# A selective-scan block with a quantised layer on one core: the direct sums of a unit ordered chunk by chunk instead of state by state

## The reference

```python
def _selective_scan(xc, delta, A, Bm, Cm, D_skip):
    dA = jnp.exp(delta[..., None] * A)
    dBx = (delta * xc)[..., None] * Bm[:, :, None, :]
    def step(h, inp):
        dA_t, dBx_t, C_t = inp
        h = dA_t * h + dBx_t
        y_t = jnp.einsum('bds,bs->bd', h, C_t)
        return (h, y_t)
    ...
    return y + D_skip * xc
...
delta = jax.nn.softplus(x_conv @ W_dt + b_dt)
y = _selective_scan(x_conv, delta, A, Bm, Cm, D_skip)
y = y * jax.nn.silu(z)
out = y @ W_out + b_out
return _layernorm(residual + out, alpha, beta)
```

## Time and profile before

| | |
|---|---|
| time, median of 3 runs | 615.03 us (614.58 to 618.79) |
| the profiled execution | 615.47 us, span of the core 613.7 us, mean granted clock of TensorE 0.94 |
| TensorE busy | 521.3 us |
| VectorE busy | 506.9 us |
| ScalarE busy | 437.3 us |
| GpSimd busy | 333.5 us |
| direct sums L1291, L1288 | 160 of 0.473 us, 32 of 0.483 us (median) |
| transposes of the states L1063 | 1024 of 0.273 us (median) |

### The profile page before, as it was taken

The page is one execution under the profiler, slowest core; times in us unless marked ns, Lnnn a source line. Parts: engine busy times, 40 slices in busy tenths (PEclk is TensorE's granted clock), DMA queues, the critical chain, the costliest instruction groups (busy, mean ns, idle before and its releaser), DMA issues.

```text
span 613.7 us, 10300 instructions
## 1 busy us (share of the span) xinstructions
PE 521.3 (85%) x2885; PEld 399.3 (65%) x2885; DVE 506.9 (83%) x1010; ACT 437.3 (71%) x882; POOL 333.5 (54%) x332
## 2 busy tenths in 40 slices
PE   7998999998999879988999789988998786962292
PEld 4566787876687757766777658776877575752031
DVE  4357799888889879898989978889989999885585
ACT  3569884988398947987598639895889586801364
POOL 3054365567365837656666735584847666501154
PEclk9999999998899999999999989999999999877555
DMA  7203351145213440445024601343053505530018
GB/s 192 49 1 69 70 104 36 36 87 102 52 27 78 91 84 1 81 90 103 1 43 98 121 15 35 68 99 73 1 103 69 103 1 103 108 66 0 1 41 200
DMA packets 20066, 41.43 MB, mean 68 GB/s; under 512 B 3760, under 2 KB 10032, under 8 KB 20016
## 3 DMA queue, kind: packets, MB, share of 16 engines
q0 software_dynamic: 10080, 35.13, 29.1%
q1 hardware_dynamic: 9936, 5.78, 3.6%
HBM read 3.68 MB, written 2.10 MB: 9 GB/s over the span
## 4 chain that ended last, share of the span: by engine, by line
PE 44%; DVE 19%; POOL 12%; issue 11%; ACT 10%; DVEq 1%; DMA 0%; POOLq 0%; ACTq 0%
PE drive L1047 14%; PE hT L1063 10%; DVE state L1268 7%; PE fbank L983 6%; PE fbank L1001 4%; DVE acc_d L1291 3%; ACT decay L785 2%; ACT nrm L696 2%; POOL u L511 2%; ACT term L806 2%; PE bbank L1081 2%; PE drive L1044 2%; POOL state L662 1%; PE drive L983 1%; PE fbank L990 1%
## 5 line engine op out<-in xcount | busy, mean ns | idle before, releaser
L1268 DVE TENSOR_TENSOR_SCAN state<-decay,drive 128x512 f32<-128x512 f32 x256 | 297.2, 1201 | 23.7 <-PE drive L1047 13.6
L785 ACT ACTIVATE decay<-delta,a_neg 128x510 f32<-128x510 f32 x256 | 170.5, 731 | 46.4 <-DVE state L1268 44.6
L1047 PE MATMUL drive<-diag,uT 128*128 128x256 f32 x768 | 186.3, 387 | 0.8 <-DVE uT L1488 0.8
L1063 PE MATMUL hT<-ident,state 128*128 128x128 f32 x1024 | 146.3, 280 | 31.2 <-DVE acc_d L1291 21.7
L1063 PEld LDWEIGHTS hT<-ident,state 128*128 128x128 f32 x1024 | 119.1, 144 | 64.0 <-issue 25.2
L1047 PEld LDWEIGHTS drive<-diag,uT 128*128 128x128 f32 x768 | 141.3, 194 | 17.6 <-DVE uT L1488 1.0
L806 ACT ACTIVATE term<-hT,Ct 128x256 f32<-128x256 f32 x256 | 102.7, 485 | 5.0 <-PE hT L1063 3.5
L538 POOL TENSOR_SCALAR_AFFINE_SELECT diag<-Bt 128x512 f32<-128x512 f32 x96 | 65.6, 713 | 34.3 <-PE drive L1047 17.5
L1291 DVE SCALAR_TENSOR_TENSOR acc_d<-hT,Ct,acc_d 128x256 f32<-128x256 f32 x160 | 66.5, 470 | 4.6 <-PE hT L1063 4.5
L523 POOL TENSOR_TENSOR scaled<-uT,Bt 128x1024 f32<-128x1024 f32 x32 | 65.5, 2048 | 8.3 <-DVE uT L1488 4.2
L554 POOL DMA_DIRECT2D acc<-term x64 | 59.9, 936 | 7.6 <-ACT term L806 6.3
(11 more groups left out here) (188 smaller groups left out, 688.1 us busy)
## 6 DMA issues: line engine op xcount, KB each, us to landing
acc<-term POOLq DMA_DIRECT2D x64, 512.0 KB, 4.5
out_dram<-x_all SPq DMA_DIRECT2D x7, 256.0 KB, 3.0
x_all<-term POOLq DMA_DIRECT2D x6, 256.0 KB, 4.1
x_all<-in_L_attn_x_dram SPq DMA_DIRECT2D x2, 256.0 KB, 4.0
state<-in_L_attn_conv_w_dram SPq DMA_DIRECT2D x1, 512.0 KB, 5.8
w_in<-in_L_attn_W_in_dram SPq DMA_DIRECT2D x1, 256.0 KB, 4.6
w_dt<-in_L_attn_W_dt_dram SPq DMA_DIRECT2D x1, 256.0 KB, 4.5
out_dram<-x_all SPq DMA_DIRECT2D x2, 128.0 KB, 2.8
```

The costliest lines, as they stand in the source:

```text
L785: last = nc.scalar.activation(decay[:, g % DECAYS, h, :, s, 1:], delta[:, par, h, :, 1:], ACT.Exp, scale=a_neg[:, h, SG * g + s:SG * g + s ...
L1047: last = nc.tensor.matmul(dst[:, :, P * c:P * c + P], uT[:, par, TC * b + c, P * h:P * h + P], diag[:, n % DIAGS, c, :, :], start=True, st ...
L1063: last = nc.tensor.transpose(hT[:, c, DI * s + P * h:DI * s + P * h + P], state[:, n % STATES, h, s, P * c:P * c + P], ident[:, :])
L1268: nc.vector.tensor_tensor_scan(state[:, n % STATES, h, :, :].rearrange("p s t -> p (s t)"), decay[:, g % DECAYS, h, b, :, :].rearrange("p ...
```

## The change

VectorE's loop over the four sums of a direct unit is turned: chunk outside, state inside. The four instructions of a unit were state 0 of chunk 0, state 0 of chunk 1, state 1 of chunk 0, state 1 of chunk 1; they become state 0 and state 1 of chunk 0, then state 0 and state 1 of chunk 1. The function directs, which tells the count at which each is done, is turned in the same way. So TensorE's wait at L1058 before bank 0 (state SG - 1, chunk 0) ends with the second sum of the unit in place of the third, and before bank 1 with the fourth as it did. VectorE's own wait at L1290 for state 0 of the same chunk now names the instruction directly in front; before, one instruction stood between. The wait for the second bank's transposes (L1286) stands before the third sum in place of the second. Everything else is as it was.

```diff
 def directs(j, s, c):
 
-    return 2 * TC * j + TC * s + c + 1
+    return 2 * TC * j + SG * c + s + 1
...
                 if j == 0 and pr.after(1):
                     dve.wait_ge(ysum_ready, nth(pr.plus(-1), PAIR, 0))
-                for s in range(SG):
-                    for c in range(TC):
+                for c in range(TC):
+                    for s in range(SG):
                         a = acc_d[:, par, b, c, :]
                         src = hT[:, c, DI * s:DI * s + DI]
                         by = Ct[:, par, TC * b + c, SG * g + s:SG * g + s + 1]
```

## The result

The changed kernel takes 624.22 us (median of 4 runs, 623.28 to 625.56) where the kernel before took 615.06 (4 runs): 1.0137 times as long, 95% interval 1.0103 to 1.0171. The forecast was 617.0 with a range of 612.0 to 620.5; the change costs 9.2 us instead of 2. The profiled execution took 625.15 us, span 623.4.

A forecast was written before the change was run, and what follows sets the result against it. TensorE (521.3 of 613.7 us busy) and VectorE (506.9) were taken to bound different stretches. Terms 2.76 + 0.20 + 0.52 - 0.28 - 1.23 = +1.97 us on the 615.03 median gave 617.0, range 612.0 to 620.5 (the forecast's own: 615.3 to 618.5).

The forecast's parts named there:

- The price of the dependence: Each direct unit on VectorE: sums waiting for the one directly in front lengthen four sums from 1.63 to 1.87, 0.23 us a unit.
- The banks: TensorE's waits for direct sums: bank 0 is freed 0.28 us earlier, but TensorE finishes 0.13 us later because of bank 1.
- The end and the late second bank: State 1 of chunk 0 fills VectorE's wait for bank 1: 1.23 us saved in pair 7's units 13 to 15, 0.28 in pair 0's unit 7.
- Pair 6: Units 12 to 15 pay 0.23 us each; GpSimd's sum L563, waiting for unit 15, comes about 0.9 later relative to unit 12.
- Off the path at zero: units 6 and 7, and the units under a busy TensorE: Units 6 and 7 of pairs 1 to 5 hide 0.3 us in a 0.41 wait; remaining units stand under never-idle TensorE: zero cost.
- The clock: Rival: shifted TensorE waits add one or two 1.5 us stretches at 0.50 (618.5 or 620.0), or remove one (615.5); chance 0.13.
- The sign that was named for a wrong path: More stretches at 0.50, or VectorE idle time gone after units 6 and 7, would make the path wrong.
- All units on the path: Rival: VectorE bounds every stretch, so all 48 direct units pay 0.23 us, 11.0 in all, giving 626.0; chance 0.07.
- The free dependence: Rival: dependent sums on VectorE still start 0.39 us apart, so only the savings remain, 2.6 us, giving 612.4; chance 0.13.

## Why the prediction was wrong

- **The price of the dependence**: right, a little small. 1.63 became 1.89, 0.26 where 0.23 was taken, and the run without it has 1.63 again. The second and the fourth sum start 0.03 behind the one in front: 331.29 + 0.46 = 331.75 and 331.78 in the changed kernel.

```profile
331.29 0.46 DVE L1288 TENSOR_SCALAR acc_d<-hT,Ct 128x256 f32<-128x256 f32 x1
331.78 0.48 DVE L1291 SCALAR_TENSOR_TENSOR acc_d<-hT,Ct,acc_d 128x256 f32<-128x256 f32 x1
```

The rule that the prediction weighed, in the Trainium skill ("VectorE: DVE Perf Modes", section "The DRAIN you can't avoid"), by which a semaphore between two VectorE operations costs nothing extra, does not hold for these instructions where the semaphore is that of the sum directly in front: 0.13 us for each.

- **The banks**: right in sign and size. At pair 3's unit 13 TensorE starts 0.26 earlier relative to VectorE (0.28 worked out) and follows with bank 1 0.16 later (0.13). The pause between the banks is 0.26, not 0.4. That the release does no harm is shown by its removal (626.0).

- **The end and the late second bank**: right. From unit 13's first sum to L1506 it is 6.62 us in place of 7.67, 1.05 saved against 1.23; pair 0's unit 7 saves 0.28 as worked out. VectorE's timeline of the changed kernel's end, against the earlier trace rows:

```profile
552.19 1.89 DVE L1291 SCALAR_TENSOR_TENSOR acc_d<-hT,Ct,acc_d 128x256 f32<-128x256 f32 x4
...
554.59 1.91 DVE L1291 SCALAR_TENSOR_TENSOR acc_d<-hT,Ct,acc_d 128x256 f32<-128x256 f32 x4
556.86 1.92 DVE L1291 SCALAR_TENSOR_TENSOR acc_d<-hT,Ct,acc_d 128x256 f32<-128x256 f32 x4 [0.36 <-PE hT L1063]
558.81 0.69 DVE L1506 TENSOR_TENSOR acc<-acc 128x512 f32<-128x512 f32 x1
```

- **Pair 6**: right. GpSimd's L563 comes 1.09 us later relative to unit 12 (14.75 against 13.66), 0.9 forecast. GpSimd's timeline before, where unit 12 starts at 480.06, and in the changed kernel, where it starts at 487.19:

```profile
493.72 1.27 POOL L563 TENSOR_TENSOR acc<-acc 128x512 f32<-128x512 f32 x1 [3.04 <-DVE acc_d L1291]
...
501.94 1.27 POOL L563 TENSOR_TENSOR acc<-acc 128x512 f32<-128x512 f32 x1 [3.71 <-DVE acc_d L1291]
```

- **Off the path at zero: units 6 and 7, and the units under a busy TensorE.** Here a step failed. The 0.41 us in front of L1311 was VectorE's wait for GpSimd's L578, and I took it as cover that stays where it is. But the later L1239 ran into L575, which takes 1.45 to 1.56 in place of 1.27, so that VectorE still waits 0.28 of the 0.41, and L1311 comes 0.19 to 0.29 later behind unit 6's first sum in each of the six pairs. (By its own price the two units were 0.46 and not 0.3, and pair 6 was not counted.) And units 12 to 15 do not end under TensorE's work alone: GpSimd waits for VectorE's statistics behind unit 14 (8.61 in place of 8.03 in pair 3's slot), or for unit 15 itself (0.22 to 0.24 in three slots), and TensorE stands idle for 0.32 to 0.38 in front of the transposes of the total, in four slots. I had looked whether TensorE is busy around these units, not who is waiting two engines on. The four steps without a costly slow stretch add up to 2.5 us where 1.05 was summed; with the idle transposes on both sides, 2.8 to 4.6 us in all where 1.97 was. These terms were too small, and were not the main miss.

- **The clock.** This is where the prediction fell. I had the mechanism, as a rival, with one or two stretches of 1.5 us and a chance of 0.13, and the sum itself held nothing for it. The profile has four more stretches between 100 and 500 us, and behind them one more and one that is twice as long. The trace before had shown that a stretch at 0.50 can follow a wait of TensorE, and that the change moves those waits. What I did not see is that the forecast itself lengthens several of them: the wait for u by 0.2 to 0.3 (1.70 to 1.71 before, 1.90 to 2.00 in five pairs), while the wait in front of unit 13, 0.43 before, is still 0.42 in two pieces and ends later. The run with the idle transposes took back 7.2 us, and the pair of runs with them on both sides leaves 2.8 to 4.6 for everything else. The sign that was named for a wrong path, more stretches at 0.50, is what came.

- **Rivals.** All units on the path, 626.0, came nearest in time, but by luck and not by its mechanism: with the idle transposes VectorE's sums take as long and the time is 617. The free dependence, 612.4, is near what the kernel without the dependence measures, 611.7. The forecast's own range, 617.0 and 1.2 more, ends at 618.2 and not at 618.5.

- **What stays open**: why the idle transposes at unit 13, and the moved L1239, also clear stretches behind other waits; where a stretch falls for a given wait; and how the loss divides between the clock and the later sums more closely than 3.8 to 6.4 against 2.8 to 4.6.

## What to carry to other kernels

Before an accumulation is reordered to release a buffer sooner, look at the distance between an instruction and the one whose result it needs: here one independent sum in between hid the whole latency; and where an engine needs all buffers at once, the last release counts, not the first. When a forecast makes a shared engine late by a few tenths of a microsecond in a kernel with a busy TensorE, go through TensorE's waits one by one and ask whether each grows, because a slow stretch behind a wait can cost far more than the wait: here the drive behind it took 1.6 us longer, for waits that grew by 0.3 or not at all. A few idle transposes in a wait can be worth more than the reordering.

## What the runs showed of the hardware

Two VectorE instructions of 0.47 us on 128x256 floats from PSUM start 0.37 to 0.40 us apart when independent and 0.49 to 0.52 apart when the second needs the first. GpSimd's multiplication of 128x512 floats takes 1.27 us alone and 1.32 to 1.61 when VectorE's elementwise minimum of 128x1024 floats in SBUF is under way at its start, the more the longer that still runs (0.18 us left: 1.32; 0.33: 1.45; 0.47: 1.61). The Trainium skill ("SBUF — State Buffer", section "Who interferes with whom") says that a VectorE instruction in a 2-port mode, which operations of this kind can enter, and GpSimd hold one pair of ports in turn, the second waiting until the first has finished. The traces agree; the length of the wait, up to 0.34 us, is these runs'. TensorE's clock fell to 1.2 GHz for the work behind waits of as little as 0.16 and 0.26 us with 1.56 before them (pair 5; two of the four pairs that have these two waits show it), and eight drive matmuls then took 3.51 us in place of 1.89 (3.44 behind the wait for u); with 0.44 us of such a wait filled with transposes it was at 2.4 GHz behind all six.
